# Recurrence steps of two middle chunks as f16 matmuls on split weight and state

## The reference, cut to what matters

```
def _L1_cond_ref(x, h0, Wx, Wh, b):
    xw = jnp.einsum('ntd,dh->nth', x, Wx) + b
    def step(prev_h, xw_t):
        next_h = jnp.tanh(xw_t + prev_h @ Wh)
        return (next_h, next_h)
    _, hs = jax.lax.scan(step, h0, jnp.swapaxes(xw, 0, 1))
    return jnp.swapaxes(hs, 0, 1)

def _L1_ffn_ref(x, router_w, w1, b1, w2, b2):
    router_logits = jnp.einsum('bth,eh->bte', x, router_w)
    topk_values, topk_indices = jax.lax.top_k(router_logits, 2)
    h1 = jax.nn.gelu(jnp.einsum('bth,efh->btef', x, w1) + b1, approximate=False)
    expert_outputs = jnp.einsum('btef,ehf->bteh', h1, w2) + b2
    ...
```

## Time and profile before

| | |
|---|---|
| median of 3 runs (lowest to highest) | 316.67 us (316.2 to 316.93) |
| the profiled execution | 315.6 us |
| its span on the core | 313.7 us |
| PE busy in the span | 260.6 us, 83% |
| DVE busy | 268.7 us, 86% |
| ACT busy | 217.6 us, 69% |
| POOL busy | 86.2 us, 27% |
| share of PE in the chain that ended last | 72% |

### The profile page before, as it was taken

How to read it: one execution, slowest core, us unless ns; L and a number is a source line. 1 busy time by engine, 2 the same in 40 slices (tenths; PEclk the granted TensorE clock), 3 DMA queues, 4 the chain that set the end, 5 groups by cost and what they waited for, 6 DMA issues and landing times.

```text
span 313.7 us, 8438 instructions
## 1 busy us (share of the span) xinstructions
PE 260.6 (83%) x2611; PEld 192.6 (61%) x2611; DVE 268.7 (86%) x644; ACT 217.6 (69%) x436; POOL 86.2 (27%) x158
## 2 busy tenths in 40 slices
PE   5779750002869899999999999999999999999994
PEld 4624340000335687778788777777777777777873
DVE  4989899989897897879998889888789888799885
ACT  6368999991243777767766677767766666688882
POOL 2787999000019712101312112212110211101000
PEclk9959957555889999999999999999999999999999
DMA  6992553100004500000000000000000000001001
GB/s 188 326 285 49 101 101 67 33 0 0 0 0 65 104 3 0 0 3 2 18 0 2 0 2 25 4 0 0 0 2 19 16 0 0 2 3 34 0 2 27
DMA packets 28122, 11.67 MB, mean 37 GB/s; under 512 B 17449, under 2 KB 27074, under 8 KB 28098
## 3 DMA queue, kind: packets, MB, share of 16 engines
q1 hardware_dynamic: 27698, 11.16, 15.1%
q10 hardware_dynamic: 400, 0.20, 0.2%
HBM read 6.11 MB, written 1.05 MB: 23 GB/s over the span
## 4 chain that ended last, share of the span: by engine, by line
PE 72%; DVE 20%; issue 2%; DMA 2%; ACT 1%; POOL 0%; ACTq 0%; SPq 0%; DVEq 0%
PE bank L845 72%; DVE peak L592 6%; DVE big L688 3%; DVE big L698 2%; DVE peak L666 2%; DMA wn<-in_w_gate 2%; DVE big L704 1%; DVE big L671 1%; DVE big L706 1%; DMA y_sb<-in_cond 1%; DVE wyT L779 0%; DVE big L824 0%; DVE c L635 0%; DVE pkm L585 0%; ACT wyT L526 0%
## 5 line engine op out<-in xcount | busy, mean ns | idle before, releaser
L553 ACT ACTIVATE big<-bank,miscT 128x384 f32<-128x384 f32 (+2 forms) x160 | 96.2, 602 | 31.7 <-PE bank L845 28.1
L845 PEld LDWEIGHTS bank<-wt,big 128*128 128x128 f16 x1536 | 97.2, 98 | 29.0 <-issue 4.3
L845 PE MATMUL bank<-wt,big 128*128 (+1 forms) x1536 | 112.9, 219 | 1.8 <-DVE big L824 0.8
L824 DVE TENSOR_TENSOR big<-big 128x384 f16<-128x384 f32 (+2 forms) x160 | 94.3, 591 | 19.9 <-ACT big L555 15.6
L845 PE MATMUL bank<-big,wt 128*128 128x384 f16 (+2 forms) x480 | 108.7, 335 | 0.2 <-POOL big L375 0.2
L845 PEld LDWEIGHTS bank<-big,wt 128*128 (+1 forms) x480 | 46.0, 116 | 12.3 <-POOL big L375 0.3
L373 POOL CAST big<-q 128x64 f16<-128x64 f32 x32 | 13.5, 422 | 132.5 <-ACT q L543 132.3
L820 DVE CAST big<-big 128x512 f16<-128x512 f32 (+2 forms) x112 | 42.3, 378 | 7.8 <-ACT big L553 5.7
L543 ACT ACTIVATE q<-bank,miscT (+1 forms) x112 | 30.6, 274 | 23.2 <-PE bank L845 22.1
L845 PE MATMUL bank<-q,wxh 128*128 (+1 forms) x254 | 44.7, 252 | 2.2 <-ACT q L515 1.6
L845 PEld LDWEIGHTS bank<-q,wxh 128*128 128x128 f32 x254 | 39.1, 192 | 7.9 <-ACT q L515 3.8
(11 more groups left out here) (147 smaller groups left out, 295.8 us busy)
## 6 DMA issues: line engine op xcount, KB each, us to landing
wnat<-in_w SPq DMA_DIRECT2D x8, 512.0 KB, 7.6
x_sb<-in_x SPq DMA_DIRECT2D x4, 256.0 KB, 4.1
out_block<-wyT SPq DMA_DIRECT2D x16, 64.0 KB
wn<-in_w_gate ACTq DMA_DIRECT2D x1, 192.0 KB, 4.9
wn<-in_w_up SPq DMA_DIRECT2D x1, 192.0 KB, 5.3
wn<-in_w_down SPq DMA_DIRECT2D x1, 192.0 KB, 5.3
b_in<-in_b SPq DMA_DIRECT2D x12, 4.0 KB
wt<-wyT SPq DMA_TRANSPOSE x8, 3.0
```

Source lines behind the costliest of these rows:

```text
L553: A(g32[:, f, 0:w], ps_h[f][:, 0:w], ACT.Gelu, bias=bias, scale=1 / WS).then_inc(g32_done, 1)
L824: V.tensor_tensor(g_lo[:, par, f, 0:w], g32[:, f, 0:w], g_hi[:, par, f, 0:w], ALU.subtract).then_inc(g_lo_done, 1)
L845: return nc.tensor.matmul(o, l, r, start=start, stop=stop, skip_group_check=True)
```

## The change

The recurrence steps of chunks 2 and 3 (steps 72 to 127, 56 of them) no longer read the f32 weight and state. Wh is split once, on POOL, into `wh_hi` and `wh_lo` in f16. POOL splits each new state of these steps by itself (`split_state`: a 128x16 cast, then a 128x16 subtraction that waits for the cast), and PE waits for the low half (`h_lo_done`) and issues four f16 matmuls of 16 columns: hi times hi, lo times hi, hi times lo, lo times lo. POOL's split of the mixing weights comes behind the 16th step of the chunk. Steps below 72 are as they were.

```
@@ gpsimd
             G.tensor_scalar(wxh[:, 1, :], wxh[:, 1, :], WS, 0.0, ALU.mult, ALU.add).then_inc(small_w, 1)
+            pool.wait_ge(small_w, 2)
...
+            pool.wait_ge(rw_done, 1)
+            link(G.tensor_scalar(wh_hi[:, :], wxh[:, 1, :], 1.0, 0.0, ALU.mult, ALU.add))
+            G.tensor_tensor(wh_lo[:, :], wxh[:, 1, :], wh_hi[:, :], ALU.subtract).then_inc(small_w, 1)
+            pool.wait_ge(small_w, 3)
             split_weights(2, 11)
...
+            def split_state(t):
+                pool.wait_ge(h32_done, t + 1)
+                at = slice(t * B, (t + 1) * B)
+                G.tensor_copy(h_hi[:, at], h32[:, at]).then_inc(h_hi_done, 1)
+                pool.wait_ge(h_hi_done, H_GROUPS + t - F16_FROM + 1)
+                G.tensor_tensor(h_lo[:, at], h32[:, at], h_hi[:, at], ALU.subtract).then_inc(h_lo_done, 1)
...
+                else:
+                    for t in range(RNN_FROM[c], min(RNN_FROM[c] + 16, to)):
+                        split_state(t)
+                    split_gates(c)
+                    for t in range(RNN_FROM[c] + 16, to):
+                        split_state(t)
@@ tensor, in pair
-                    if step is not None:
+                    if step is not None and c >= F16_CHUNK:
+                        pe.wait_ge(h_lo_done, step + (H_GROUPS - F16_FROM))
+                        to, state = bass.ds(rnn_column(c, step), B), bass.ds((step - 1) * B, B)
+                        mm(ps_rnn[:, to], wh_hi[:, :], h_hi[:, state], False)
+                        mm(ps_rnn[:, to], wh_lo[:, :], h_hi[:, state], False)
+                        mm(ps_rnn[:, to], wh_hi[:, :], h_lo[:, state], False)
+                        mm(ps_rnn[:, to], wh_lo[:, :], h_lo[:, state], False).then_inc(rnn_mm, 1)
+                    elif step is not None:
                         pe.wait_ge(h32_done, step)
                         mm(ps_rnn[:, bass.ds(rnn_column(c, step), B)], w_h32, h32[:, bass.ds((step - 1) * B, B)],
                            False).then_inc(rnn_mm, 1)
```

More of the change, by code:

```diff
@@ L49 @@
 W_CHUNKS = 2 * E
+F16_CHUNK = 2
+F16_FROM = RNN_FROM[F16_CHUNK]
+H_GROUPS = F16_FROM // 4
 SIG_V = 2
@@ L106, in program @@
         wx_lo = sb("wx_lo", [P, P], F16)
+        wh_hi = sb("wh_hi", [P, P], F16)
+        wh_lo = sb("wh_lo", [P, P], F16)
         NM = E * NF + 1 + E
@@ L406, in _ @@
             for c in range(CH):
[L407 to L414, removed]
+                to = RNN_FROM[c + 1] if c < CH - 1 else T
+                if c < F16_CHUNK:
+                    for i in range(done, min(done + 3, to // 4)):
+                        split_states(i)
+                    split_gates(c)
+                    for i in range(min(done + 3, to // 4), to // 4):
+                        split_states(i)
+                    done = to // 4
+                else:
+                    for t in range(RNN_FROM[c], min(RNN_FROM[c] + 16, to)):
+                        split_state(t)
+                    split_gates(c)
+                    for t in range(RNN_FROM[c] + 16, to):
+                        split_state(t)
         @block.scalar
@@ L952, in _ @@
                 if c == 2:
-                    pe.wait_ge(small_w, 2)
+                    pe.wait_ge(small_w, 3)
                     pe.wait_ge(x1_lo_done, 1)
@@ L1036, in pair @@
                     if first and s == 0:
-                        pe.wait_ge(h_lo_done, START[c + 1] // (4 * B))
+                        steps = START[c + 1] // B
+                        pe.wait_ge(h_lo_done, steps // 4 if steps <= F16_FROM else H_GROUPS + steps - F16_FROM)
                     t = slice(START[c], START[c + 1])
```

## The result

The changed kernel takes 334.75 us (median; 333.1 to 335.34) against 316.8 for the kernel before: ratio 1.0563, 95% interval 1.0528 to 1.0599. It is 17.95 us slower. The forecast was 330.2 us, in a range of 320 to 336.

A forecast was written before the change was run, and what follows sets the result against it. PE's queue was taken to bound the loops of chunks 2 and 3. Loops 7.6 + 4.5, constant-address pairs 0.9 and POOL's other work 0.5 made 13.5 us on 315.6: 329.1, by the median 330.2 us; range 320 to 336.

The forecast's parts named there:

- the sum's own mechanism: Chunks 2 and 3: PE waits for POOL's chain, whose cast DVE's subtraction locks; 326 to 334 us, chance 0.60.
- rival 3: Address instructions or a second lock, on POOL's subtraction, make each step 0.1 to 0.2 us longer: 335 to 340 us, chance 0.12.
- PE is the bound, and a wait in its queue is lost in full: Loops of chunks 2 and 3: PE is busy throughout, so a microsecond of waiting put into its queue is lost.
- 0.10 us a step won on PE: Recurrence steps: four f16 pairs cost 0.10 us against 0.20 for f32; over 56 steps 5.6 us.
- The chain through POOL is longer than the slot even when free: Loop of chunk 2: tanh, cast, subtraction and next load sum to 1.57 us, against a slot of 1.41 us.
- the address instructions of the new matmuls: On PE behind the wait: 0 to 0.2 us per waiting step, 0 to 8 us in all; taken as 0.
- The lock: DVE's two-input SBUF subtraction holds POOL's cast until 0.09 us after its end; slots settle near 1.80 us.
- locked always: Loop of chunk 2: POOL's next cast falls inside DVE's subtraction for every slot length from 1.44 to 2.13 us.
- The pairs with constant addresses: Pairs outside the loops: free chain about 1.2 us, lock remains; chunk 2 about +0.3 us, chunk 3 about +0.6.
- POOL's other work: `split_gates` before the 17th step of each chunk: +0.5 us for both, bounds 0 and 2; split of Wh hidden.
- POOL mostly misses the lock: Rival: phases settle so POOL mostly misses DVE's subtraction and the free chain holds; 319 to 326 us, chance 0.18.
- The clock did not fall: Rival: PE waits so much that its granted clock falls to 1.2 GHz; about 400 us, chance 0.02.

The follow-up runs named there:

- e10: Changed kernel, chunks 2 and 3 written out, f32 gelu kept in PSUM, f = 1's f16 half on ACT, gelus reordered, nothing left out: 310.95 us, 0.9849 of before.
- e1: Changed kernel, but the f16 matmuls read the split state of eight steps earlier and PE waits only for the newest tanh: 314.29 us, 0.9928 of before.
- e7: Changed kernel with pairs of chunks 2 and 3 written out and DVE's subtraction reading PSUM, low-half gelu left out: 314.39 us, 0.9937 of before.
- e9: As e7, but ACT's second gelu of f = 3 in chunks 2 and 3 comes behind the next slot's tanh: 313.08 us, 0.9900 of before.
- e5: Changed kernel, but the four f16 matmuls always read columns 0 to 15, an address known at build: 330.33 us, 1.0441 of before.
- e2: Changed kernel, but DVE's low-half subtraction reads PSUM instead of g32, low-half gelu left out: 323.79 us, 1.0240 of before.

## Why the prediction was right, and where a term was off

The time lies in the stated range and the kernel became slower for the reason that was given. It lies outside the narrower interval for the sum's own mechanism (326 to 334 us), and 0.25 us below that of rival 3 (335 to 340). The sum was 4.55 us short. By the starts of the tanhs, the terms came out so: first pair of chunk 2 +1.8 us (forecast 0.3), its loop +8.8 (7.6), first pair of chunk 3 +0.6 (0.6), its loop +7.0 (4.5, and 0.5 for `split_gates`).

**PE is the bound, and a wait in its queue is lost in full:** right. The whole difference lies where the queue now waits.

**0.10 us a step won on PE:** right in size. The slot of e10 is 1.41 to 1.42 us against 1.51. But it is won in full only in a kernel in which the tanh is never late either; with f = 3's two gelus ahead of it, e1 and e7 got 2.9 and 2.6 us over the two stretches, and e9 1.7 us more than e7.

**The chain through POOL is longer than the slot even when free:** right, and under-sized. I had 1.57 us; in after, where the casts are free, tanhs mostly follow at 1.67 to 1.70. The mis-sized term is the one for the address instructions of the new matmuls, which I took as nothing (bounds 0 to 8 us). They are 0.03 us more from POOL to the load (0.27 instead of 0.24) and 0.05 more from load to tanh (0.56 instead of 0.51); e5, which takes them and some of the old ones away, is worth 4.4 us. The reason that I gave, that addresses which recur cost nothing a second time, holds only within each pair of matmuls (221.32 to 221.35): the hi and lo half of the state lie at two addresses.

**The lock:** the mechanism was right, down to the end of a held cast (DVE ends at 219.87 + 0.69 = 220.56, the cast at 220.62, 0.06 later, where I took 0.09). Not right was "locked always". The casts alternate: a held one delays the next step so much that its cast meets only the tail of DVE's subtraction, and slots are 1.67 and 2.04 us by turns, not 1.80. The sum needs only every second cast held, so it survives this: from a load to the load after next it is 3.72 us (217.47 to 221.19) where I had 3.59. Of the difference 0.12 is the address instructions again: the gelu starts 1.22 us behind the load instead of 1.10 (1.09 in e5, 208.79 to 209.88), and DVE's subtraction ends 3.09 behind it instead of 2.97. Rounds are 7.54 us (1.81 + 2.02 + 1.67 + 2.04) instead of 7.30 in chunk 2, and mostly 6.82 to 6.88 instead of 6.59 in chunk 3. An estimate from these, 0.24 us for each of 12 rounds, is 2.9 us of the 4.5 us by which the sum was short.

**The pairs with constant addresses:** the other mis-sized term. From the tanh of step 72 to that of step 80 it went from 12.50 to 14.27 us, 1.8 and not 0.3; chunk 3's is 0.6, as forecast. I had the lock act there without working it through. Done as for the loop, with 0.41 for the gelu's start behind the last wide matmul and 0.1 from POOL to the load, the load after next comes 3.35 us after a load, slots of 1.67; measured are 1.59 to 1.82 for the first seven, and 2.46 for the last, on the way into the loop. But from the sixth step on the holders are others than I had (timeline of after):

```profile
189.35 0.41 DVE L843 CAST big<-big 128x512 f16<-128x512 f32 x1
...
189.45 0.37 POOL L390 CAST big<-q 128x16 f16<-128x16 f32 x1 [0.69 <-ACT q L566]
...
189.79 0.69 DVE L847 TENSOR_TENSOR big<-big 128x512 f16<-128x512 f32 x1
189.90 0.67 POOL L392 TENSOR_TENSOR big<-q,big 128x16 f16<-128x16 f32 x1
```

DVE's cast holds POOL's cast, and then DVE's subtraction holds POOL's subtraction for 0.67 instead of 0.22 us. That is the second lock of rival 3. Over both chunks it acts on 8 of POOL's 56 subtractions, six of them in the first pairs. e2 takes DVE's subtraction out of the lock, and this pair falls to 12.01.

**POOL's other work:** under-sized, within its bounds. In chunk 3 the `split_gates` stands between two steps and makes one interval 2.70 instead of 1.67 us, so it costs 1.0 us and not 0.5; in chunk 2 it is hidden. The split of Wh, 0.31 and 0.43 us at 29 us, has POOL's idle behind it.

**Rivals.** That POOL mostly misses the lock did not come true: 34 of 56 casts are held. Rival 3 was in large part true: the free chain is 0.10 to 0.13 us longer than summed, and the second lock exists, if rarely. That the time is still in the range owes something to how wide the range was. The clock did not fall.

## What to carry to other kernels

Before a conversion is put between two steps of a recurrence, add up the whole loop from one step's weight load to the next, with every engine's waiting and address instructions in it, and compare it with the slot of the engine that sets the time; here 0.10 us won on PE was paid with a chain of 1.7 us, against a slot of 1.41. A small GpSimd operation that falls on VectorE's cast or two-input subtraction in SBUF ends only after it (0.20 us became 0.58 here), so in a chain either let VectorE read from PSUM, as e10 does, or split the state elsewhere; the latter no run tried. And a loop's address instructions, free on an engine that never waits, become latency on one that does: writing the loop out changed nothing in the kernel before and took 8.5 us off the kernel after.

## What the runs showed of the hardware

VectorE's plain cast from SBUF holds GpSimd too. In e7, where the subtraction no longer does, 9 of the 56 casts still last over 0.3 us. This one is held by a cast of DVE (209.33 + 0.41 = 209.74) and ends 0.06 us after it (timeline of e7):

```profile
209.33 0.41 DVE L848 CAST big<-big 128x512 f16<-128x512 f32 x1
...
209.43 0.37 POOL L395 CAST big<-q 128x16 f16<-128x16 f32 x1 [0.91 <-ACT q L571]
```

I had worked with the subtraction alone. The Trainium skill, "SBUF — State Buffer", "SBUF: two separate sides", names both kinds of holder, two SBUF inputs and a mode that uses two ports. The trace agrees that a subtraction of the first kind and this cast both hold POOL; in which mode the cast ran it does not show. From PSUM the same cast takes longer but holds nothing. In e10's loop it is 0.68 us instead of 0.41, and a cast of POOL under it takes 0.20:

```profile
206.09 0.68 DVE L865 CAST big<-bank 128x512 f16<-128x512 f32 x1
...
206.27 0.20 POOL L395 CAST big<-q 128x16 f16<-128x16 f32 x1 [0.92 <-ACT q L573]
```
